# Eight instead of four front rows before the block barrier, and the biases spread by one transfer ahead of it

## What is computed

```python
# part 1, token by token in order: S is the state of a head
o = r_t . (S + u * k_t v_t);  S = decay_t * S + k_t v_t
x = x + ga * (token mixing and feed-forward of layernorm(x))
# part 2
gate_logits = einsum('btd,ed->bte', h, Wg)          # h: layernorm(x) * (1 + cb) + sb
topk_val, topk_idx = top_k(softmax(gate_logits), 2) # normalised to sum 1
for e in range(E):
    hh = einsum('btd,hd->bth', h, W1[e]) + b1[e]    # 512 numbers, b1 is the bias
    a, b = split(hh, 2)
    out = out + (a * sigmoid(b) @ Wo.T + bo) * comb[..., e:e+1]
x = x + gb * out
```

## Time and profile before

| | |
|---|---|
| three runs | 734.57, 736.35, 737.39 us; median 736.35 |
| the profiled execution | 735.61 us, of which the span (first to last instruction) is 733.9 |
| TensorE busy | 624.6 us (85% of the span), mean granted clock 0.941 |
| VectorE, ScalarE, GpSimd busy | 602.1, 517.0, 536.0 us |
| the barrier between the blocks | at about 473 us of the span |

### The profile page before, as it was taken

One profiled execution on the slowest core, in us unless ns is written; L12 is line 12 of the kernel. 1 busy time (PEld: TensorE's weight loads), 2 busy tenths in 40 slices (PEclk: granted clock), 3 DMA queues, 4 the chain that ended last, 5 costly groups with the idle time before them and its releaser, 6 DMA issues. The chain is left out here.

```text
span 733.9 us, 14250 instructions
## 1 busy us (share of the span) xinstructions
PE 624.6 (85%) x3527; PEld 476.9 (65%) x3527; DVE 602.1 (82%) x1384; ACT 517.0 (70%) x1309; POOL 536.0 (73%) x657
## 2 busy tenths in 40 slices
PE   3667789999999799979897877438699999999994
PEld 1434556667777567756664775416588888888884
DVE  6389999999999999989999545644578888888884
ACT  2656688889888787878576666713278888888883
POOL 5466668899999769899879765364766666666666
PEclk9978999999999999999998998858899999999998
DMA  3998898899999879779789796247355444444530
GB/s 109 254 139 126 116 135 128 135 149 143 163 139 148 136 123 140 149 154 182 125 152 166 189 317 187 73 126 225 85 79 83 76 77 80 82 81 82 85 70 1
DMA packets 104308, 95.58 MB, mean 130 GB/s; under 512 B 14635, under 2 KB 82822, under 8 KB 104102
## 3 DMA queue, kind: packets, MB, share of 16 engines
q1 hardware_dynamic: 85702, 77.60, 57.3%
q0 software_dynamic: 16176, 12.75, 9.7%
q10 hardware_dynamic: 2352, 4.33, 1.8%
HBM read 35.47 MB, written 25.61 MB: 83 GB/s over the span
## 5 line engine op out<-in xcount | busy, mean ns | idle before, releaser
L2065 POOL DMA_INDIRECT out<-res,index x91 | 141.6, 1556 | 75.3 <-DVE res L2146 57.9
L833 POOL TENSOR_TENSOR rs_prod<-rT,state_rows 128x512 f32<-128x512 f32 x128 | 139.1, 1096 | 39.9 <-DVE state_rows L1518 38.4
L1513 DVE TENSOR_TENSOR kv<-key,v_spread 128x512 f32<-128x512 f32 x128 | 84.7, 671 | 11.9 <-DMA v_spread<-vT 9.0
L1518 DVE TENSOR_TENSOR_SCAN state_rows<-decay,state_rows,kv 128x512 f32<-128x512 f32 x64 | 79.7, 1265 | 0.0
L1518 DVE TENSOR_TENSOR_SCAN state_rows<-decay,kv 128x512 f32<-128x512 f32 x64 | 75.8, 1202 | 0.0
L1271 PEld LDWEIGHTS ps_k<-w,gel 128*128 128x128 f32 x512 | 64.1, 207 | 16.6 <-issue 12.8
L1271 PE MATMUL ps_k<-w,gel 128*128 128x128 f32 x512 | 66.8, 293 | 2.4 <-ACT gel L1088 2.4
L1980 ACT ACTIVATE sig<-ps_a 128x256 f32<-128x256 f32 x91 | 34.9, 384 | 47.4 <-issue 20.6
L2113 DVE SCALAR_TENSOR_TENSOR half<-ps_b,xg,sig 128x256 f32<-128x256 f32 x91 | 43.6, 479 | 25.6 <-ACT sig L1984 22.3
L1236 PE MATMUL ps_f<-hnT_hi,mix_hi 128*128 128x512 f32 x128 | 55.7, 435 | 6.7 <-DVE hnT_lo L1641 5.5
L2106 DVE SCALAR_TENSOR_TENSOR ps_a<-ps_a,xg,sig 128x256 f32<-128x256 f32 x91 | 44.3, 487 | 15.4 <-ACT sig L1980 10.5
(11 more groups left out here) (354 smaller groups left out, 1895.1 us busy)
## 6 DMA issues: line engine op xcount, KB each, us to landing
v_spread<-vT SPq DMA_DIRECT2D x128, 256.0 KB, 5.3
xg<-sorted_scratch SPq DMA_DIRECT2D x91, 130.0 KB
xin<-in_L_attn_x SPq DMA_DIRECT2D x16, 256.0 KB, 6.3
x<-in_L_attn_x SPq DMA_DIRECT2D x16, 256.0 KB, 5.4
out<-x SPq DMA_DIRECT2D x16, 256.0 KB
sorted_scratch<-gel SPq DMA_DIRECT2D x4, 910.0 KB, 8.3
tokens_scratch<-h SPq DMA_DIRECT2D x12, 256.0 KB
raw_w<-in_L_ffn_W ACTq DMA_DIRECT2D x2, 1024.0 KB, 9.5
```

The source lines that it names most:

```text
L833: pool.tensor_tensor(rs_prod[:, p, idx % 4], rT[p][:], state[idx][:, p * NT:(p + 1) * NT], ALU.mult).then_inc(s["rs_ready"], 1)
L1513: dve.tensor_tensor(kv[idx % 2][:], key[:], v_spread[idx % SPREADS][:], ALU.mult).then_inc(s["kv_ready"], 1)
L1518: dve.tensor_tensor_scan(state[idx][:, 1 + p * NT:1 + (p + 1) * NT], decay[:], kv[idx % 2][:], first, ALU.mult, ALU.add) \
L2065: pool.indirect_dma_start(out_rows, bass.IndirectOffsetOnAxis(ap=index[k % RESULTS][:, i:i + 1], axis=0), res[k % RESULTS][:, i, :], None, ...
```

## The change

Four edits that belong together.

1. `FRONT_EARLY` goes from 4 to 8: eight front rows are stored in the token block and four by `list_front`.
2. `bias_rows` is kept from the token block on. It lies in memory that eight tiles of the token block (`lora`, `ruk`, three `gate`, two `bonus`, one `kv`) take up until the recurrence ends; they are now called `room`.
3. SyncE fills it with one transfer of 2 MB (`load_bias_rows`, 128 partitions by 16 KB) ahead of iteration 22, after waits for the last reader of the old tiles; the eight transfers of ScalarE go, and with them the wait for them.
4. `FIRST_SEED` goes from 10 to 2: ScalarE seeds from the third group on.

```diff
-IN_FRONT, FRONT_EARLY = 12, 4
+IN_FRONT, FRONT_EARLY = 12, 8
...
+        with nc.sbuf_tensor("bias_rows", [P, E * H2], F32) as bias_rows:
+            pass
+        room = [keep.enter_context(nc.sbuf_tensor(f"room{i}", [P, NT], F32)) for i in range(E * H2 // NT)]
...
-        lora = sb("lora", [P, NT])
-
-        ruk = sb("ruk", [P, NT])
-        gate, bonus = ([sb(f"{n}{i}", [P, NT]) for i in range(n_)] for n, n_ in (("gate", GATES), ("bonus", 2)))
-        kv = [sb(f"kv{i}", [P, NT]) for i in range(2)]
+        lora, ruk = room[0:2]
+        gate, bonus = room[2:2 + GATES], room[2 + GATES:4 + GATES]
+        kv = [room[4 + GATES], sb("kv1", [P, NT])]
...
+        BIAS_ROWS_AT = TILES + 6
...
+            def load_bias_rows():
+
+                sp.wait_ge(s["ogated_ready"], TILES)
+                sp.wait_ge(s["scan_ready"], TILES * DK)
+                sp.dma_start(bias_rows[:], ins["L0_ffn_b1"].rearrange("e h -> (e h)").unsqueeze(0).broadcast_to([P, E * H2])).then_inc(s["bias_rows_in"], 16)
+
...
-            run_pipeline(step, {CLEAR_AT: store_blank, BIAS_AT + 1: store_bias, ROWS_AT: load_last_rows, SPREAD_AT: spread_bias})
+            run_pipeline(step, {CLEAR_AT: store_blank, BIAS_AT + 1: store_bias, BIAS_ROWS_AT: load_bias_rows, ROWS_AT: load_last_rows, SPREAD_AT: spread_bias})
...
+            sp.wait_ge(s["bias_rows_in"], 16)
...
-    FIRST_SEED = 10
+    FIRST_SEED = 2
...
-            def load_bias():
-
-                for e in range(E):
-                    act.dma_start(bias_rows[:, e * H2:(e + 1) * H2], ins["L0_ffn_b1"][e:e + 1, :].broadcast_to([P, H2])).then_inc(s["bias_in"], 16)
-
...
-                    if j == FIRST_SEED:
-                        act.wait_ge(s["bias_in"], 16 * E)
...
-                if k == 0:
-                    load_bias()
```

More of the change, by code:

```diff
@@ L349, in build @@
         v_spread = [keep.enter_context(nc.sbuf_tensor(f"v_spread{i}", [P, NT], F32)) for i in range(E // 2)]
+        with nc.sbuf_tensor("bias_rows", [P, E * H2], F32) as bias_rows:
+            pass
+        room = [keep.enter_context(nc.sbuf_tensor(f"room{i}", [P, NT], F32)) for i in range(E * H2 // NT)]
         assert E * H2 == 8 * NT
         kept = (w_hi, w_lo, out_w, logits, expert_rank, tags, state_rows, last_rows, dest, below, ones, starts, codes, pair_steps, column, row_table, pair_table,
-                work, done, at, hits, mask, sel, pos, tot, off, carry_on, small, share, rs_prod, bias_all, v_spread, early_groups, late_groups, EARLY)
+                work, done, at, hits, mask, sel, pos, tot, off, carry_on, small, share, rs_prod, bias_all, v_spread, bias_rows, room, early_groups, late_groups, EARLY)
         rows_listed = nc.alloc_semaphore("rows_listed")
@@ L369, in attention_block @@
     (w_hi, w_lo, out_w, logits, expert_rank, tags, state_rows, last_rows, dest, below, ones, starts, codes, pair_steps, column, row_table, pair_table,
-     work, done, at, hits, mask, sel, pos, tot, off, carry_on, small, share, rs_prod, bias_all, v_spread, early_groups, late_groups, early) = kept
+     work, done, at, hits, mask, sel, pos, tot, off, carry_on, small, share, rs_prod, bias_all, v_spread, bias_rows, room, early_groups, late_groups, early) = kept
     NH2 = out_w.shape[1]
@@ L446, in attention_block @@
         out_w_rows = exp_w[:, 0:out_w.shape[1] * P]
-        lora = sb("lora", [P, NT])
-        ruk = sb("ruk", [P, NT])
-        gate, bonus = ([sb(f"{n}{i}", [P, NT]) for i in range(n_)] for n, n_ in (("gate", GATES), ("bonus", 2)))
-        kv = [sb(f"kv{i}", [P, NT]) for i in range(2)]
+        lora, ruk = room[0:2]
+        gate, bonus = room[2:2 + GATES], room[2 + GATES:4 + GATES]
+        kv = [room[4 + GATES], sb("kv1", [P, NT])]
+        assert len(room) == 5 + GATES
         state = [state_rows[:, i * PITCH + SKEW:i * PITCH + SKEW + 1 + TPB * NT] for i in range(DK)]
@@ L490, in attention_block @@
             "shift1_ready shift2_ready scan_ready rs_ready kv_ready ln2_stats ln2_mv ln2_ve ln2_rstd xn4_ready h3_scaled h3_ready h3T_ps h3T_ready logits_ps logits_ready "
-            "small_ps small_ready expert_in expert_ps expert_hi expert_lo b1_ready b1_stored bias_in route_step tag_step rows_gated batch_staged tags_kept gain_ready exps_ready ranks_ps totals_ps totals_ready unlisted_ready blank_stored last_staged gates_in gates_spread tags_set out_w_in listed table_step table_ps").split(),
+            "small_ps small_ready expert_in expert_ps expert_hi expert_lo b1_ready b1_stored bias_in route_step tag_step rows_gated batch_staged tags_kept gain_ready exps_ready ranks_ps totals_ps totals_ready unlisted_ready blank_stored bias_rows_in last_staged gates_in gates_spread tags_set out_w_in listed table_step table_ps").split(),
             {"early_in": 2, "late_in": 2, "x_loaded": 2, "xre_loaded": 2, "x2_stored": 2, "h3_stored": 2, "staged": 2, "listed": 2, "v_spread": SPREADS,
@@ L1828, in expert_block @@
             "small_in parts_set xT_ps xT_hi_ready xT_lo_ready a_ps b_ps sig_a_ready sig_b_ready half_ready glu_a glu_b glu_ready "
-            "gT_ps gT_ready y_ps biased res_ready lo_set listed table_step tables_set left_set bias_in low_seeded seeded "
+            "gT_ps gT_ready y_ps biased res_ready lo_set listed table_step tables_set left_set low_seeded seeded "
             "route_step gain_ready exps_ready totals_ps totals_ready ranks_ps tag_step").split(),
```

1 line of the change is left out of this document (removed).

## The result

The changed kernel takes 733.21 us in the median of 20 runs (727.95 to 735.28), beside 736.31 for the kernel before in the median of 20 (732.19 to 741.58). The ratio is 0.9948, with a 95% interval of 0.9925 to 0.9970: by it the change is worth 3.8 us (2.2 to 5.5; the medians differ by 3.1), where 9.0 were forecast.

A forecast was written before the change was run, and what follows sets the result against it. TensorE was taken to bound the expert block's middle, and barrier, eight stores and gather to set its start. Gains of 3.6 + 3.1 + 0.5 + 0.5 + 1.0 = 8.7 us off 735.6 gave 726.9, 727.3 by medians; range 720 to 733.

The forecast's parts named there:

- Four stores cross the barrier: At the seam of the blocks: 5.74 us leave the chain behind the barrier, which moves 2.1 us later; gain 3.6 us.
- The collision of the spread with the rows: Ahead of the barrier: the spread, 451 to 461 us, holds GpSimd's rows; ScalarE's first split starts at 464, not 462.1.
- The second and fourth rival: Second: spread ends at 465, ScalarE's splits 4 us later, 731 us, chance 0.10; fourth: ends at 475, 741 us, 0.04.
- The eight issues leave ScalarE: Group 0: ScalarE's second gate starts 3.1 us earlier, and group 2's first product comes at 500.1 us; gain 3.1 us.
- Bias matmuls and seeds: Groups 2 to 9: twelve matmuls leave TensorE; 0.5 us won at groups 2 and 3, 0.5 at pair 4.
- The clock: From 504.4 to 507.8 us: the fall to 1.2 GHz may not come; 1.0 us won, bounds 0 and 1.5.
- a sign against it: The forecast is wrong if the low clock appears in a stretch where it was high.
- The gap ahead of group 10: TensorE's 5.84 us stop up to 531.88 us: forecast to stay at 5 to 6; rival, it vanishes, 722.3 us, chance 0.15.

The follow-up runs named there:

- e3_seed10: The changed kernel with ScalarE's seeds from group 10 on, as before the change; 722.74 us, ratio 0.9902.
- e14: The changed kernel, but each of GpSimd's last twenty row stores is issued only once the one before it has landed; 747.49 us.
- e15: The changed kernel with seeds from group 10 on, twelve late rows instead of eight ahead of the first scatter and four behind it; 731.74 us, ratio 0.9919.
- e16: The changed kernel with seeds from group 10 on, late rows still eight ahead of the first scatter and eight behind it; 734.59 us, ratio 0.9945.
- e5_before: The kernel before, with nothing changed, run once more for its trace; 735.92 us in the median, 734.85 us in the trace.
- e1_front8: The kernel before with FRONT_EARLY at 8 instead of 4 and no other part of the change; 726.49 us, ratio 0.9958.
- e2_spread: The kernel before with only the one-transfer spread of the biases, four early front stores and seeds from group 10 on; 729.21 us, ratio 0.9987.
- e9: The changed kernel, with nothing altered, run again beside the kernel before; 722.77 us, ratio 0.9883.
- e10: The changed kernel with seeds from group 10 on, a second time; 721.78 us, ratio 0.988.
- e13: The changed kernel with GpSimd's sixteen late row stores moved behind the fifth pair's scatter; 748.17 us.

## Why the prediction was wrong

Forecast 727.3 us, range 720 to 733; the median is 733.2.

- **Four stores cross the barrier, 3.6 us: right.** 4.1 in the trace, 3.1 alone by the clock. The barrier moved by 1.6 us (2.1 foreseen), by GpSimd's stores alone: they end at 475.16, ScalarE's last split at 472.84.
- **The collision of the spread with the rows: its size was wrong, and its mechanism held in part.** GpSimd's queue stood still beside the spread until 454 us. From then on the two queues took turns: 24 of SyncE's packets to 23 of GpSimd's from 455 to 456 us, 22 to 22 from 456 to 457. In e3_seed10, whose spread was issued 3.3 us earlier, they did so from 452 us on; the rows of the queues from 453 to 454 us:

```profile
q1 hardware_dynamic: 24, 0.39, 92.8%
q0 software_dynamic: 22, 0.08, 19.5%
```

  That is what the Trainium skill says (page "DMA: Bandwidth & Descriptors", section "Queues, rings and completion order": the engines take the queues in turn, packet by packet), so these traces agree with it for as long as both queues have packets there. What it does not account for are the stretches without any packet of GpSimd's, three us here and seven beside bias_all; what holds the queue there is open. The prediction made those seven us the rule. It had also taken the rate from bias_all, 0.21 MB a us; the measured one is 0.41. The first split came early, not late. The second and fourth rival rested on this and did not come.
- **The eight issues leave ScalarE, 3.1 us: the price came, the step behind it failed.** The trace shows 3.0 us more at group 2. What failed is the tacit step that TensorE's pace from group 2 on stays as it was. With the issues gone, ScalarE is 4.7 us late at group 2, and the way from group 2 to 4 takes 9.4 us, where it took 6.9 in the kernel before; 5.4 (6.9 less 0.5 for the seeds and 1.0 for the clock) would have met the forecast. The runs show that the cause is GpSimd's piled stores (e14 beside e15 and e16), and that it is not the seeds (e16 has none there and is late). I had seen the same late starts ahead of group 10 and priced only whether they go, not whether new ones appear.

  Why the kernel before has none at groups 2 and 3 is not shown. While ScalarE issued its transfers, from 496.2 to 501.0 us, GpSimd was in its eight stores (495.44 to 505.26), and the issues may have covered the stop. But its two gates of group 2, the next ones that wait for a new product, come 0.04 and 0.03 us behind their products:

```profile
504.17 0.38 ACT L1980 ACTIVATE sig<-ps_a 128x256 f32<-128x256 f32 x1 [1.94 <-DVE glu L2122]
505.53 0.39 ACT L1984 ACTIVATE sig<-ps_b 128x256 f32<-128x256 f32 x1 [0.98 <-issue]
```

  In the changed kernel the stop opens 5.3 us behind the first store and ends 2.5 us behind the last; at the same distances it would lie from 500.7 to 506.8 us here. e5_before, the other trace of this kernel, has no late gate there either. And the eight issues take no longer on a stalling chip (4.73 us, 4.97 in e5) than on a calm one (5.81 in e1_front8). So it may as well be that the transfers themselves keep the stop away. e1_front8 or e2_spread on a stalling chip would tell; both ran on a calm one only.
- **Bias matmuls and seeds, 1.0 us: mis-sized, nothing is won.** On the clock it is 0.9883 with the seeds, 0.988 without. From group 2 to 12 it takes 27.5 us with seeds and 27.0 without (e9, e10): pairs 1 and 4 win 0.8 and 0.35 us, and pairs 2 and 3 lose 0.9 and 0.8, where I had written that the seeds "are covered and win nothing". This is the 1.6 us between groups 4 and 8 in the books above. There the join comes late for VectorE's table steps, and behind it now stands a copy of 0.60 us instead of a matmul of 0.23.
- **The clock, 1.0 us: not won.** The fall from 504.4 to 507.8 us did not go, it moved and grew, from 3.4 us to 4.5. TensorE had stood still again (2.76 us up to 503.88), and the granted clock reads 0.50, which is 1.2 GHz, from 505.5 to 510 us. It was high from 507.8 to 510 before, which the prediction had named as a sign against it.
- **The gap ahead of group 10: stayed**, with 0.15 on its going; 4.38 us, where 5 to 6 were foreseen. It is the same stall, under the second batch of eight stores.
- **On a calm chip the sum comes out: 8.5 us (5.7 to 11.4) where 8.7 were foreseen.** Without the stall the change is thus worth about what was forecast, but the agreement is in part luck. Two of its terms, the seeds and the clock, 2.0 us, are not seen to be won in any trace. And GpSimd's chain from the first scatter on sets the time there, which the prediction didn't have; the gain passes through since the first scatter moves with the start of the block.

Open: which resource stalls ScalarE. It is not the load of the DMA engines as a whole: in the kernel before their share reads 1.05 from 504.4 to 507.8 us and no gate is over 0.1 us late, and in the changed one it reads 0.40 from 496.2 to 505.6, where ScalarE is late. The waits that came late are on TensorE's signals, and ScalarE's engine had nothing to do; whether the signal or ScalarE's instructions came late, no run tells apart. Open too is what sets the two kinds of chips or occasions apart.

## What to carry to other kernels

Before a wait or an issue is taken off an engine, look at what else runs there, on the other engines as well: here 3 us were taken off ScalarE's path, and 2.5 us of late starts appeared right behind. A stop in the profile that no wait explains is to be looked for on another chip before a gain is counted on either side of it. And a queue that feeds two consumers in order (row stores, then scatters) is to be laid out by who waits for each entry: on calm chips four late stores moved ahead of the first scatter went with 4 to 6 us, while the seeds were worth nothing.

## What the runs showed of the hardware

- Two kinds of chips or occasions: the kernel before takes 736 to 738 us in three of the six sets of runs and 729 to 732 in the three others, each set on one chip. The front stores of the traced kernels start some 4 us earlier on the calm ones (459.2 to 461.7 us in ten traces, 462.5 to 466.4 in nine, with one of 460.5, e13, on a stalling chip), and only on the stalling ones is ScalarE late.
- On stalling chips single gates of ScalarE are up to 9.2 us late (e16, group 8) when eight indirect stores of 128 rows of 1,040 bytes are issued at a pitch of 1.27 us, and up to 3.3 us late (e15, group 8) when it is four. It starts some 3 to 7 us behind the first of them and ends 1 to 6 us behind the last. The stores of e14, 2.7 to 4.0 us apart, don't do it, nor do the first eight late ones in the two traces of the kernel before, beside ScalarE's eight transfers.
- The transfer of 16 KB pieces from the input into 128 partitions moved 0.41 MB a us; the two from the kernel's scratch buffer, 64 partitions each, moved 0.21. They differ in source and in width, and no run parts the two. GpSimd's queue moved nothing beside the second for seven us, nothing for three us beside the first, and then took turns with it, one packet for one.
